# Square layers of a tiled attention and feed-forward kernel: a 16-bit low part, a power-of-two lift, and products of a kind in runs of 16

## Chip, cores and metric

The kernel runs on one core of a Trainium2 chip. The metric is the device time of one execution in microseconds; the kernel before was run three times: 905.81, 905.95 and 906.56 us, median 905.95.

## What is computed

Two blocks with residuals over x (32 sequences of 128 rows, 256 features): cross attention with 8 heads whose source is the normalised x and whose target is a context, then a feed-forward part whose weights hold only -1, 0 and 1 and a scale per output.

```python
x = x + xattn(ctx, layernorm(x), mask, mask, ...)          # all float32
def ffn(x):                                                # x: layernorm of the above, 256 features
    h = silu((x @ w1.T) * s1) * ((x @ w2.T) * s2)          # gates: 256 -> 1024
    h = gelu((h @ h1.T) * t1)                              # layer one:  1024 -> 1024
    h = gelu((h @ h2.T) * t2)                              # layer two:  1024 -> 1024
    return (h @ w3.T) * s3                                 # output: 1024 -> 256
x = x + ffn(layernorm(x))
```

## The kernel before

The sequences go through in 16 tiles of two, 256 rows each. Activations stand feature by row, so a product has a 128x128 block of a weight as the stationary operand and 128x256 of activations as the moving one; a layer of 1024 to 1024 is 8 output blocks of 8 steps. While tile f is in its feed-forward part, tile f+1 finishes its attention and f+2 starts it. The order of work is written out by hand for each engine (`tile`, `gates_part`, `middle_part`); tiles 1 to 12 are a hardware loop, tile 0 and tiles 13 to 15 stand apart. On TensorE a loop tile is: the four gate groups (`gate_up`), the projections of keys, queries and values of tile f+2 (L488, L506, L524), layer one, then attention, scores and output projection (L614, L542, L631), layer two, the output layer (`ffn_out`, L767). Engines meet by semaphores, whose targets `at` works out from the tile's number.

Since the weights are exact in few bits, float32 activations are kept by splitting them: VectorE casts a value to F32R (the high part, `hi`) and subtracts that from the value (the low part, `lo`). `split(f, q)` does this for a pair of 128x256 blocks, L1312 and L1314; q 0 to 3 is the gates' result, 4 to 7 layer one's, 8 to 11 layer two's. Each weight block is multiplied with both parts into one bank of PSUM. In the two square layers and the output layer both parts are F32R and alternate:

```python
for k in ks:
    part_product(mid_bank(f, q)[:, half, :], W, k, cols, hi, k == 0, False, general)
    ins = part_product(mid_bank(f, q)[:, half, :], W, k, cols, lo, False, k == KH - 1, general)
```

In the gates (L639, L640) the low part is F16 (`x2q`), multiplied with the upper 16 bits of each weight, two steps or four of a kind in a row; there the LayerNorm's result is 2**22 times too large, so that the low part keeps clear of F16's smallest values, and `gscols` takes it back. ScalarE does Silu (L891), Gelu (L898) and the exponentials (L926); GpSimd the power for LayerNorm and, at the start, casts of the weights. In tile 0 ScalarE also looks at every chunk of weights (L985) for bits below the 16th, and a flag chooses between the program above and one in float32 (`general`); with these inputs the first runs.

Of the kernel before, what the change touches and what calls it, by code (L numbers as in the profile page):

```python
# [19 lines left out]
LIFT = 2.0 ** 22  # L20
CH = 1024
# [11 lines left out]
    xt_done=1, k_done=2, q_done=1, v_done=1, xnT_ready=1, xnO_ready=1, kT_ready=2, qT_ready=2, vb_ready=1, v_ready=2,  # L33
# [8 lines left out]
def program(nc, x, ctxT, mask_row, mask_col, wsT, wvT, wtT, woT, first_rows, second_rows, x_mask_1, w1T, w2T, h1T, h2T,  # L42
            w3T, out):
    st = ExitStack()
    with st:
# [24 lines left out]
        neg_half = sb("neg_half", [P, NB])  # L70
# [27 lines left out]

        def turned(buf):

            return buf[:].rearrange("p c t -> p (c t)").rearrange("p (a c j i) -> p a c j i", a=ROWS, c=KD, j=NB)
# [5 lines left out]
        hAh, hAl = sb("hAh", [P, KH, T], F32R), sb("hAl", [P, KH, T], F32R)  # L107
# [6 lines left out]
        gscols = sb("gscols", [P, 2 * KH])  # L114

# [48 lines left out]
        def mid_bank(f, q):  # L164

            if q in (6, 10) and isinstance(f, int) and (f == TILES - 1 or f in (0, TILES - 2) and q == 6):
                return G[0][:].rearrange("p (h t) -> p h t", h=2)
            return F[q % 2][:]

# [64 lines left out]
        gscols_ready = sem("gscols_ready")  # L234
        gate_done = sem("gate_done")
# [81 lines left out]
        def _(sp):  # L317
# [54 lines left out]

            def store(f):
# [5 lines left out]
            def tile(f, a, m):  # L379
# [11 lines left out]
                if a is not None:  # L391
                    turn_x2(a)
                if m is not None:
                    turn_x(m)
# [62 lines left out]
        def _(pe):  # L457
# [248 lines left out]
            def middle_steps(f, q, half, ks, general):  # L706

                W, hi, lo = ((H1, H1_raw), hAh, hAl) if q < 8 else ((H2, H2_raw), hBh, hBl)
# [169 lines left out]
        def _(act):  # L878
            fn = nc.scalar.activation

            def silu(f, q):
# [105 lines left out]

            def tile(f, a, n):
# [54 lines left out]
            tile(0, 1, 2)  # L1043
            with act.Fori(1, TILES - 3) as i:
# [7 lines left out]
        def _(dve):  # L1052
# [232 lines left out]
            def gate_times_up(f, q):  # L1285
# [322 lines left out]
```

## Time and profile before

| | |
|---|---|
| median of three executions | 905.95 us |
| the profiled execution's own time | 906.56 us |
| its span, first to last instruction | 904.7 us |
| TensorE busy | 899.1 us, 99% |
| VectorE busy | 626.5 us, 69% |
| ScalarE busy | 390.6 us, 43% |
| GpSimd busy | 76.9 us, 8% |
| chain that ended last, by engine | PE 95%, DVE, DMA, POOL, ACT and issue 1% each |

The busy time of an engine counts its instructions, not its waits. The chain is followed back from the last instruction, at each step to what released it; its pieces on TensorE give the time that a run of products really takes, since single products overlap in the pipeline (one lasts some 280 ns and the next starts about 117 later).

### The profile page before, as it was taken

To read this page: it belongs to the slowest core of one execution; us is meant where nothing else is said; L and a number is where in the kernel's file an instruction comes from. 1 tells how busy PE (TensorE), PEld (TensorE's weight loads), DVE (VectorE), ACT (ScalarE), POOL (GpSimd) and SP (SyncE) were. 2 spreads that over 40 slices of the span, in tenths; PEclk is the share of its full clock that TensorE was granted. 3 is DMA by queue.
4 is the path that set the end of the run, shared out by engine and by line. 5 is a ranking of instruction groups with operands and counts; after the bars stand their busy time and mean duration, and the time that the engine had idled before them with its cause. 6 is when DMAs were issued, how large, how long until landed. Compare 5 with 4: busy or idle time off the path is not lost.

```text
span 904.7 us, 20863 instructions
## 1 busy us (share of the span) xinstructions
PE 899.1 (99%) x7600; PEld 853.8 (94%) x7600; DVE 626.5 (69%) x1256; ACT 390.6 (43%) x1101; POOL 76.9 (8%) x101
## 2 busy tenths in 40 slices
PE   9999999999999999999999999999999999999998
PEld 7799999999999999999999999999999999999998
DVE  5888858577585776858668586785857758586453
ACT  5973524425253252623535235253443525355231
POOL 3544000010000100001010000100001000000000
PEclk9999999999999999999999999999999999999999
DMA  9932232412214232142411424113241231303000
GB/s 347 385 116 57 75 81 62 122 56 85 74 46 122 65 100 60 36 122 70 119 37 35 122 70 122 39 55 98 70 122 47 75 87 54 94 24 106 24 13 14
DMA packets 82352, 79.27 MB, mean 88 GB/s; under 512 B 8592, under 2 KB 74896, under 8 KB 82320
## 3 DMA queue, kind: packets, MB, share of 16 engines
q1 hardware_dynamic: 81744, 78.31, 28.2%
q10 hardware_dynamic: 576, 0.52, 0.2%
q8 instruction: 21, 0.34, 0.2%
q14 instruction: 11, 0.09, 0.0%
HBM read 51.55 MB, written 27.26 MB: 87 GB/s over the span
## 4 chain that ended last, share of the span: by engine, by line
PE 95%; DVE 1%; DMA 1%; POOL 1%; ACT 1%; issue 1%; SPq 0%; DVEq 0%; POOLq 0%; ACTq 0%
PE F L646 50%; PE F L767 7%; PE G L631 6%; PE G L488 6%; PE G L524 5%; PE F L640 3%; PE G L640 3%; PE F L639 3%; PE G L639 3%; PE G L506 2%; PE S L542 2%; PE G L614 2%; PE G L646 1%; PE F L524 1%; DMA pr<-p_dram 0%
## 5 line engine op out<-in xcount | busy, mean ns | idle before, releaser
L898 ACT ACTIVATE g<-F,firsts 128x256 f32<-128x256 f32 x248 | 104.0, 472 | 320.6 <-PE F L646 317.7
L646 PE MATMUL F<-hBh,H 128*128 128x256 f32 x1008 | 239.5, 283 | 0.1
L646 PE MATMUL F<-hBl,H 128*128 128x256 f32 x1008 | 236.4, 279 | 0.0
L646 PE MATMUL F<-hAh,H 128*128 128x256 f32 x976 | 231.8, 282 | 0.0
L646 PE MATMUL F<-hAl,H 128*128 128x256 f32 x976 | 228.8, 279 | 0.0
L646 PEld LDWEIGHTS F<-hBl,H 128*128 128x128 f32 x1008 | 190.0, 188 | 0.4
L646 PEld LDWEIGHTS F<-hBh,H 128*128 128x128 f32 x1008 | 189.0, 187 | 0.7 <-ACT g L898 0.3
L646 PEld LDWEIGHTS F<-hAl,H 128*128 128x128 f32 x976 | 183.9, 188 | 0.4
L646 PEld LDWEIGHTS F<-hAh,H 128*128 128x128 f32 x976 | 183.0, 188 | 0.8 <-ACT sil L891 0.4
L1312 DVE CAST hBh<-g 128x512 fp32r<-128x512 f32 x64 | 28.1, 440 | 118.3 <-ACT g L898 118.3
L926 ACT ACTIVATE pr<-pr,nmx 128x128 f32<-128x128 f32 x240 | 92.7, 387 | 0.2
L1314 DVE TENSOR_TENSOR hAl<-g,hAh 128x512 fp32r<-128x512 f32 x128 | 88.6, 692 | 4.4
L1312 DVE CAST hAh<-g 128x512 fp32r<-128x512 f32 x128 | 54.9, 429 | 33.0 <-ACT g L898 31.8
L1479 POOL TENSOR_TENSOR rs<-ve,neg_half 128x2 f32<-128x2 f32 x15 | 10.4, 693 | 647.5 <-DVE ve L1246 647.5
L767 PE MATMUL F<-W,hAh 128*128 128x256 f32 x256 | 61.3, 281 | 0.0
L767 PE MATMUL F<-W,hAl 128*128 128x256 f32 x256 | 61.2, 280 | 0.0
L898 ACT ACT_TABLE_LOAD x17 | 21.8, 1283 | 76.6 <-PE F L646 76.6
L640 PE MATMUL F<-x2h,W 128*128 128x256 f32 x256 | 51.5, 302 | 0.5 <-DVE g L1293 0.5
L640 PE MATMUL G<-x2h,W 128*128 128x256 f32 x256 | 51.2, 301 | 0.0
L524 PE MATMUL G<-WV,cT 128*128 128x256 f32 x224 | 50.6, 379 | 0.0
L488 PE MATMUL G<-cT,WK 128*128 128x256 f32 x224 | 50.6, 379 | 0.0
L891 ACT ACTIVATE sil<-G,gscols 128x256 f32<-128x256 f32 x64 | 26.9, 471 | 53.4 <-PE G L640 53.4
(163 smaller groups left out, 1452.3 us busy)
## 6 DMA issues: line engine op xcount, KB each, us to landing
p_dram<-pb SPq DMA_DIRECT2D x30, 512.0 KB, 3.3
pr<-p_dram SPq DMA_DIRECT2D x120, 128.0 KB, 3.2
H_raw<-h SPq DMA_DIRECT2D x16, 512.0 KB, 14.5
cT<-ctx_t SPq DMA_DIRECT2D x14, 512.0 KB, 3.5
x_dram<-xt SPq DMA_DIRECT2D x28, 256.0 KB, 2.4
out<-y SPq DMA_DIRECT2D x32, 128.0 KB, 1.8
x_in<-x_t SPq DMA_DIRECT2D x15, 256.0 KB, 2.7
x2T<-x_dram SPq DMA_DIRECT2D x60, 64.0 KB, 1.9
```

The lines of the kernel that those rows point to most:

```text
L488: ins = mm(k_part(a, c), WK[:, k, c * P:(c + 1) * P], cT_of(a)[:, k, :], start=k == 0, stop=k == KC - 1)
L524: ins = mm(v_bank(a)[:, j * D:(j + 1) * D], cT_of(a)[:, k, j * P:(j + 1) * P], WV[:, k, :], start=k == 0, stop=k == KC - 1)
L631: ins = mm(G[1][:, j * D:(j + 1) * D], lhsT, WO[:, k, :], start=k == 0, stop=k == 2 * KD - 1)
L639: return mm(bank, high_halves(W[0])[:, k, cols], x2q[:, k, :], start=first, stop=last)
L640: return mm(bank, W[0][:, k, cols], x2h[:, k, :], start=first, stop=last)
L646: return mm(bank, W[0][:, k, cols], part[:, k, :], start=first, stop=last)
L767: ins = mm(F[j][:, 0, :], lhsT, W3[:, k, :], start=first, stop=last)
L891: fn(sil[:, p % 4, :], gate_bank[:, p % 2, :], ACT.Silu, scale=gscols[:, p:p + 1]).then_inc(sil_ready, 1)
L898: fn(g[:, q % 2, m, :], mid_bank(f, q)[:, m, :], ACT.Gelu, scale=scols[:, col:col + 1]).then_inc(gelu_ready, 1)
L926: ins = fn(pr[j][:, r, c, :], pr[j][:, r, c, :], ACT.Exp, bias=nmx[:, j, h:h + 1], scale=SCALE, accum_out=den[:, j, h:h + 1])
L1312: V.tensor_copy(hi[:, pair, :], g[:, q % 2, :, :]).then_inc(hi_ready, 1)
L1314: V.tensor_tensor(lo[:, pair, :], g[:, q % 2, :, :], hi[:, pair, :].bitcast(F32), ALU.subtract).then_inc(h_ready, 1)
```

## The change

In tiles 1 to 15 the low part of the two square layers is F16 (`hAq`, `hBq`) and is multiplied with the upper 16 bits of the weights. To keep it in range the layers' inputs are multiplied by powers of two: the gates' through the columns of scales that they are multiplied with anyway, layer one's by a multiplication of its own on VectorE ahead of each split (L1395), and Gelu's scales take both back (`lifted_cols`). The powers come from bounds that the kernel works out in tile 0: ScalarE squares and sums 12 chunks of weights, VectorE reduces these and the scales, the results go through memory to all partitions, and GpSimd and VectorE make the factors. Silu and Gelu write into `gA` and `gB`, which lie where `hAl` and `hBl` lie, instead of a ring of four and of two. The low and high steps of an output block are done in runs, and the order turns from block to block. Tile 0 and the output layer multiply as before.

```diff
+        hAh = sb("hAh", [P, KH, T], F32R)
+        hAl, gA = with_raw("hAl", KH, T)
         hBh, tile1_home = with_raw("hBh", KH, T)
-        hBl = sb("hBl", [P, KH, T], F32R)
-        g, sil = sb("g", [P, 2, 2, T]), sb("sil", [P, 4, T])
+        hBl, gB = with_raw("hBl", KH, T)
+        at_byte = -(-nc.sbuf_base // 32) * 32
+        hAq = sb("hAq", [P, KH, T], F16)
+        g = nc.alloc_sbuf_tensor_at("g", [P, 2, 2, T], F32, offset=at_byte)
+        hBq = sb("hBq", [P, KH, T], F16)
...
+        def g_pair(f, q):
+
+            if q >= 8 or is_first(f):
+                return g[:, q % 2]
+            return (gA, gB)[q // 4][:, 2 * (q % 4):2 * (q % 4) + 2, :]
...
+            def spread_sizes():
+
+                sp.wait_ge(sizes_ready, 3)
+                sp.dma_start(sizes_dram, sizes).then_inc(sizes_written, 16)
...
+                sp.dma_start(all_sizes, sizes_dram.rearrange("p n -> (p n)").unsqueeze(0).broadcast_to([P, 6 * P])).then_inc(sizes_loaded, 16)
...
-                for k in ks:
-                    if m == 0 and k % 2 == 0:
-                        pe.wait_ge(h_ready, at("h_ready", f, q - 4 + k // 2 + 1))
-                    cols = slice(m * P, (m + 1) * P)
-                    part_product(mid_bank(f, q)[:, half, :], W, k, cols, hi, k == 0, False, general)
-                    ins = part_product(mid_bank(f, q)[:, half, :], W, k, cols, lo, False, k == KH - 1, general)
...
+                else:
+                    lows = (half == 1, half == 0)
+                    for low in lows:
+                        for k in ks:
+                            first, last = low == lows[0] and k == 0, low == lows[1] and k == KH - 1
+                            if m == 0 and k % 2 == 0:
+                                done, name = (h_ready, "h_ready") if low else (hi_ready, "hi_ready")
+                                pe.wait_ge(done, at(name, f, q - 4 + k // 2 + 1))
+                            if low:
+                                ins = mm(bank, high_halves(W[0])[:, k, cols], low16[:, k, :], start=first, stop=last)
+                            else:
+                                ins = mm(bank, W[0][:, k, cols], hi[:, k, :], start=first, stop=last)
...
-                    if not isinstance(f, int):
-                        act.wait_ge(g_ready, at("g_ready", f, max(p - 3, 0)))
                     act.wait_ge(gate_done, at("gate_done", f, q + 1))
-                    if isinstance(f, int) and (f or p > 3):
-                        act.wait_ge(g_ready, at("g_ready", f, max(p - 3, 0)))
-                    fn(sil[:, p % 4, :], gate_bank[:, p % 2, :], ACT.Silu, scale=gscols[:, p:p + 1]).then_inc(sil_ready, 1)
+                    if is_first(f) and q > 1:
+                        act.wait_ge(h_ready, q - 1)
+                    fn(g_pair(f, q)[:, p % 2, :], gate_bank[:, p % 2, :], ACT.Silu, scale=gscols[:, p:p + 1]).then_inc(sil_ready, 1)
 
             def gelu(f, q):
-                act.wait_ge(h_ready, at("h_ready", f, q - 1))
+                if is_first(f) or q > 9:
+                    act.wait_ge(h_ready, at("h_ready", f, q - 1))
                 act.wait_ge(mid_done, at("mid_done", f, q - 3))
                 for m in (0, 1):
                     col = KH + 2 * q + m
-                    fn(g[:, q % 2, m, :], mid_bank(f, q)[:, m, :], ACT.Gelu,
-                       scale=scols[:, col:col + 1]).then_inc(gelu_ready, 1)
+                    scale = scols[:, col:col + 1] if is_first(f) else lifted_cols[:, col - KH:col - KH + 1]
+                    fn(g_pair(f, q)[:, m, :], mid_bank(f, q)[:, m, :], ACT.Gelu, scale=scale).then_inc(gelu_ready, 1)
...
+            def sum_squares(ns):
+
+                for n in ns:
+                    _, _, W = chunks[n]
+                    act.wait_ge(squares_ready, n)
+                    fn(y[:].rearrange("p j n -> p (j n)").bitcast(BF16)[:, 0:CH], W.rearrange("p k m -> p (k m)").bitcast(F32), ACT.Square,
+                       accum_out=squares[:, n:n + 1]).then_inc(squares_ready, 1)
...
+                    if first and q == 5:
+                        act.wait_ge(raw_loaded, 80)
+                    if first and q in (5, 6, 7):
+                        sum_squares(((0, 1), (2, 3), (4, 5))[q - 5])
...
+                    if first and q == 7:
+                        sum_squares(range(6, 10))
...
+                    if first and q == 8:
+                        sum_squares((10, 11))
...
+            act.wait_ge(lifted_cols_ready, 3)
...
-                dve.wait_ge(h_ready, at("h_ready", f, max(q - 1, 0)))
+                scales = gscols[:, KH:2 * KH] if is_first(f) else lifted_cols[:, 0:KH]
                 for p in (2 * q, 2 * q + 1):
+                    gate = g_pair(f, q)[:, p % 2, :]
                     dve.wait_ge(sil_ready, at("sil_ready", f, p + 1))
-                    V.scalar_tensor_tensor(g[:, q % 2, p % 2, :], up_bank[:, p % 2, :], gscols[:, KH + p:KH + p + 1],
-                                               sil[:, p % 4, :], ALU.mult, ALU.mult).then_inc(g_ready, 1)
+                    V.scalar_tensor_tensor(gate, up_bank[:, p % 2, :], scales[:, p:p + 1],
+                                               gate, ALU.mult, ALU.mult).then_inc(g_ready, 1)
...
+                if q < 8 and not is_first(f):
+                    lo = (hAq, hBq)[q // 4]
...
+                if 4 <= q < 8 and not is_first(f):
+                    V.tensor_scalar(whole_g, whole_g, lift[:, 1:2], None, ALU.mult).then_inc(in_lift, 1)
+                    dve.wait_ge(in_lift, at("in_lift", f - 1, q - 3))
+                V.tensor_copy(hi[:, pair, :], whole_g).then_inc(hi_ready, 1)
                 dve.wait_ge(hi_ready, at("hi_ready", f, q + 1))
-                V.tensor_tensor(lo[:, pair, :], g[:, q % 2, :, :], hi[:, pair, :].bitcast(F32),
+                V.tensor_tensor(lo[:, pair, :], whole_g, hi[:, pair, :].bitcast(F32),
...
+            def size_columns():
+
+                dve.wait_ge(squares_ready, BOUNDED)
+                gates = squares[:, 0:2 * KD].rearrange("p (w k) -> p w k", w=2)
+                V.tensor_reduce(sizes[:, 0:2], gates, AX.X, ALU.add).then_inc(sizes_ready, 1)
+                V.tensor_reduce(sizes[:, 2:3], squares[:, 2 * KD:], AX.X, ALU.add).then_inc(sizes_ready, 1)
...
+                V.tensor_reduce(sizes[:, 3:6], lifted_cols.rearrange("p (w k) -> p w k", w=3), AX.X, ALU.max).then_inc(sizes_ready, 1)
+
+            def lift_from_sizes():
+
+                dve.wait_ge(sizes_loaded, 16)
+                each = all_sizes.rearrange("p (s n) -> p n s", n=6)
+                V.tensor_reduce(whole[:, 0:3], each[:, 0:3], AX.X, ALU.add).then_inc(lift_steps, 1)
+                V.tensor_reduce(whole[:, 3:6], each[:, 3:6], AX.X, ALU.max).then_inc(lift_steps, 1)
...
+                V.tensor_tensor(whole[:, 0:3], whole[:, 0:3], whole[:, 3:6], ALU.mult).then_inc(whole_ready, 1)
+
+            def lift_columns():
+
+                dve.wait_ge(inverse_roots, 1)
+                V.scalar_tensor_tensor(lift[:, 0:1], whole[:, 3:4], ROOM / 16.0 ** 2, whole[:, 4:5], ALU.mult, ALU.mult).then_inc(lift_steps, 1)
...
+                V.tensor_scalar(lift.bitcast(I32), lift.bitcast(I32), 0x7F800000, None, ALU.bitwise_and).then_inc(lift_steps, 1)
...
+                V.tensor_scalar(lifted_cols[:, 0:KH], gscols[:, KH:2 * KH], lift[:, 0:1], None, ALU.mult).then_inc(lifted_cols_ready, 1)
...
+                V.tensor_scalar(lifted_cols[:, 2 * KH:3 * KH], scols[:, 3 * KH:4 * KH], unlift[:, 1:2], None, ALU.mult).then_inc(lifted_cols_ready, 1)
+                dve.wait_ge(lifted_cols_ready, 3)
...
                     mask_scores(n, 1)
+                if first:
+                    row_max(n, 1)
+                    size_columns()
                 split(f, 9)
...
                 split(f, 11)
-                if n is not None:
+                if first:
+                    lift_from_sizes()
+                elif n is not None:
                     row_max(n, 1)
                 scale_out(f, 0)
                 if a is None:
                     add_residual(f, 0)
                 scale_out(f, 1)
+                if first:
+                    lift_columns()
                 if a is not None:
...
+            pool.wait_ge(whole_ready, 1)
+            Gp.tensor_tensor(whole[:, 3:6], whole[:, 0:3], neg_half[:], ALU.pow).then_inc(inverse_roots, 1)
```

TensorE, entry into layer one of a loop tile, before (L646 is a product of either part; F0 is a PSUM bank, H1 the weights):

```order
L524 MATMUL G1<-WV,cT 128x256 x8
L688 REGISTER_ALU
L712 ISA
L646 MATMUL F0<-hAh,H1 128x256
L646 MATMUL F0<-hAl,H1 128x256
```

and now (L778 high, L776 low), from the last two steps of the first block's high run on:

```order
L778 MATMUL F0<-hAh,H1 128x256 x2
L776 MATMUL F0<-hAq,H1 128x256 x16
L778 MATMUL F0<-hAh,H1 128x256 x8
L778 MATMUL F1<-hAh,H1 128x256 x8
L776 MATMUL F1<-hAq,H1 128x256 x16
L778 MATMUL F1<-hAh,H1 128x256 x8
```

A pair of high and low, with a weight block loaded for each, has become 8 high, 16 low, 16 high and so on; the waits are on the high part first.

VectorE, the first split of layer one's result in a loop tile, before (L1312 the cast, L1314 the subtraction):

```order
L1197 STREAM_TRANSPOSE pb1<-pr1 128x8x4x32
L1305 REGISTER_ALU
L1306 ISA
L1312 CAST hBh<-g 128x512
L1313 REGISTER_ALU
L1314 TENSOR_TENSOR hBl<-g,hBh 128x512
```

and now (L1395 is the multiplication by the lift):

```order
L1276 STREAM_TRANSPOSE pb1<-pr1 128x8x4x32
L1387 REGISTER_ALU
L1388 ISA
L1395 TENSOR_SCALAR hBl_raw_58<-hBl_raw_58,small 128x512
L1396 ISA
L1397 CAST hBh<-hBl_raw_58 128x512
L1398 REGISTER_ALU
L1399 TENSOR_TENSOR hBq<-hBl_raw_58,hBh 128x512
```

One instruction and a wait on it stand ahead of the cast; the low part goes to `hBq`.

VectorE in tile 0, from split 8 to split 9, before (L1128 masks scores, L1063 begins tile 3's LayerNorm):

```order
L1314 TENSOR_TENSOR hAl<-g,hAh 128x512
L1128 TENSOR_TENSOR pr1<-S,mbias 128x1024
L1312 CAST hAh<-g 128x512
L1314 TENSOR_TENSOR hAl<-g,hAh 128x512
L1063 BN_STATS st1<-x_in 128x6 x2
```

and now (L1211 and L1215 are the maximum over scores, L1406 to L1410 `size_columns`):

```order
L1399 TENSOR_TENSOR hAl<-g_59,hAh 128x512
L1207 TENSOR_TENSOR pr1<-S,mbias 128x1024
L1211 TENSOR_REDUCE mx<-pr1 128x8
L1215 TENSOR_SCALAR nmx<-mx 128x8
L1406 TENSOR_REDUCE small<-small 128x2
L1407 TENSOR_REDUCE small<-small 128x1
L1408 TENSOR_TENSOR small<-firsts 128x24
L1410 TENSOR_REDUCE small<-small 128x3
L1397 CAST hAh<-g_59 128x512
L1399 TENSOR_TENSOR hAl<-g_59,hAh 128x512
```

The maximum over scores has moved here from behind split 11, where `lift_from_sizes` now stands, and four small instructions have come in between.

## Rows read from the trace of the kernel before

**Rows 1.** Page, totals: span, then busy us, share, instructions.

```profile
span 904.7 us, 20863 instructions
PE 899.1 (99%) x7600; PEld 853.8 (94%) x7600; DVE 626.5 (69%) x1256; ACT 390.6 (43%) x1101; POOL 76.9 (8%) x101
```

**Rows 2.** Chain that ended last, a loop tile: start us, us, what.

```profile
219.28 14.93 PE F L646 x128
...
239.97 14.94 PE F L646 x128
...
258.69 0.23 PE G L640 x2
258.92 0.45 PE G L639 x4
259.38 0.47 PE G L640 x4
...
266.10 3.45 PE G L488 x16
```

**Rows 3.** Line L639, the gates' low products: duration ns min/median/max.

```profile
L639 PEld LDWEIGHTS G<-x2q,W x256: 96/98/101, 34.1 to 864.8; 128*128 128x128 bf16 x128
L639 PE MATMUL G<-x2q,W x256: 272/273/284, 34.1 to 864.9; 128*128 128x256 f16 x128
```

**Rows 4.** Timeline of TensorE, two low products of a run: start, length.

```profile
96.34 0.38 PE L639 MATMUL G<-x2q,W 128*128 128x256 f16 x2
```

**Rows 5.** The chain in tile 14.

```profile
832.47 4.14 DMA pr<-p_dram
836.61 0.04 issue
836.66 0.65 PE G L614 x16
```

**Rows 6.** Timeline of VectorE, a loop tile; in brackets idle time before, releaser.

```profile
225.36 0.43 DVE L1312 CAST hBh<-g 128x512 fp32r<-128x512 f32 x1 [1.42 <-ACT g L898]
...
231.45 0.43 DVE L1312 CAST hBh<-g 128x512 fp32r<-128x512 f32 x1 [2.58 <-ACT g L898]
...
240.07 0.69 DVE L1237 TENSOR_TENSOR x<-G,xb 128x512 f32<-128x512 f32 x1 [0.99 <-PE G L631]
...
264.73 0.87 DVE L1293 SCALAR_TENSOR_TENSOR g<-G,gscols,sil 128x256 f32<-128x256 f32 x2
```

**Rows 7.** Groups of VectorE by line: busy us, mean ns, idle before.

```profile
L1078 DVE TENSOR_SCALAR xn<-x_in,mv,rs 128x256 f32<-128x256 f32 x30 | 11.0, 410 | 12.0 <-POOL rs L1467 12.0
L1246 DVE TENSOR_SCALAR ve<-mv 128x2 f32<-128x2 f32 x15 | 2.5, 170 | 1.6
L1160 DVE TENSOR_REDUCE mx<-pr 128x4 f32<-128x512 f32 x4 | 2.7, 686 | 0.1
L1263 DVE TENSOR_TENSOR x2l<-x2T,x2h 128x256 fp32r<-128x256 f32 x30 | 11.3, 420 | 0.0
L1263 DVE TENSOR_TENSOR x2q<-x2T,x2h 128x256 f16<-128x256 f32 x30 | 10.9, 404 | 0.1
```

**Rows 8.** Timeline of ScalarE, tile 0.

```profile
45.88 1.09 ACT L985 ACTIVATE look_out<-H_raw 128x1024 bf16<-128x1024 uint16 x1
...
77.45 0.84 ACT L898 ACTIVATE g<-F,firsts 128x256 f32<-128x256 f32 x2 [5.05 <-PE F L646]
```

**Rows 9.** Timeline of VectorE, tile 0 and the start of tile 1.

```profile
63.06 1.41 DVE L1314 TENSOR_TENSOR hBl<-g,hBh 128x512 fp32r<-128x512 f32 x1
...
81.02 1.22 DVE L1128 TENSOR_TENSOR pr<-S,mbias 128x1024 f32<-128x1024 f32 x1
...
89.98 0.69 DVE L1314 TENSOR_TENSOR hAl<-g,hAh 128x512 fp32r<-128x512 f32 x1
...
94.43 0.88 DVE L1293 SCALAR_TENSOR_TENSOR g<-G,gscols,sil 128x256 f32<-128x256 f32 x2 [0.51 <-PE G L640]
```

**Rows 10.** The chain in tile 0, its output layer.

```profile
88.55 3.78 PE F L767 x32
```

**Rows 11.** DMA issues: count, KB each, median us from issue to landing.

```profile
firsts<-mask_row SPq DMA_DIRECT2D x14, 128.0 KB, 3.2
```

More of the change, by code:

```diff
@@ L20 @@
 LIFT = 2.0 ** 22
+ROOM = 2.0 ** 26
+BOUNDED = 2 * KD + KH
 CH = 1024
@@ L69, in program @@
         ident = sb("ident", [P, P])
-        neg_half = sb("neg_half", [P, NB])
+        neg_half = sb("neg_half", [P, 3])
         act_set = sb("act_set", [P, 1])
@@ L97, in program @@
         x2_dram = nc.dram_tensor("x2_dram", (ROWS, P, KD * NB * DH), F32, kind="Internal").ap()
+        sizes_dram = nc.dram_tensor("sizes_dram", (P, 6), F32, kind="Internal").ap()
+        all_sizes = pb[0][:].rearrange("p s n -> p (s n)")[:, 0:6 * P]
         def turned(buf):
@@ L114, in program @@
         gscols = sb("gscols", [P, 2 * KH])
+        small = sb("small", [P, 3 * KH + BOUNDED + 16])
+        lifted_cols, squares = small[:, 0:3 * KH], small[:, 3 * KH:3 * KH + BOUNDED]
+        sizes, lift = small[:, 3 * KH + BOUNDED:3 * KH + BOUNDED + 6], small[:, 3 * KH + BOUNDED + 6:3 * KH + BOUNDED + 8]
+        unlift = small[:, 3 * KH + BOUNDED + 8:3 * KH + BOUNDED + 10]
+        whole = small[:, 3 * KH + BOUNDED + 10:3 * KH + BOUNDED + 16]
         cT_1 = tile1_home[:, 0:KC, :]
@@ L168, in mid_bank, with is_first @@
             return F[q % 2][:]
+        def is_first(f):
+            return isinstance(f, int) and f == 0
+        def g_pair(f, q):
+            if q >= 8 or is_first(f):
+                return g[:, q % 2]
+            return (gA, gB)[q // 4][:, 2 * (q % 4):2 * (q % 4) + 2, :]
         def sem(name):
@@ L234, in program @@
         gscols_ready = sem("gscols_ready")
+        squares_ready = sem("squares_ready")
+        sizes_ready = sem("sizes_ready")
+        scales_squared = sem("scales_squared")
+        sizes_written = sem("sizes_written")
+        sizes_loaded = sem("sizes_loaded")
+        whole_ready = sem("whole_ready")
+        inverse_roots = sem("inverse_roots")
+        lift_steps = sem("lift_steps")
+        lifted_cols_ready = sem("lifted_cols_ready")
+        in_lift = sem("in_lift")
         gate_done = sem("gate_done")
@@ L392, in tile @@
                     turn_x2(a)
+                if is_first(f):
+                    spread_sizes()
                 if m is not None:
@@ L706, in middle_steps @@
             def middle_steps(f, q, half, ks, general):
-                W, hi, lo = ((H1, H1_raw), hAh, hAl) if q < 8 else ((H2, H2_raw), hBh, hBl)
+                W, hi, lo, low16, whole_g = (((H1, H1_raw), hAh, hAl, hAq, gA) if q < 8 else ((H2, H2_raw), hBh, hBl, hBq, gB))
                 m = 2 * (q % 4) + half
-                for k in ks:
-                    if m == 0 and k % 2 == 0:
-                        pe.wait_ge(h_ready, at("h_ready", f, q - 4 + k // 2 + 1))
-                    cols = slice(m * P, (m + 1) * P)
-                    part_product(mid_bank(f, q)[:, half, :], W, k, cols, hi, k == 0, False, general)
-                    ins = part_product(mid_bank(f, q)[:, half, :], W, k, cols, lo, False, k == KH - 1, general)
+                cols = slice(m * P, (m + 1) * P)
+                bank = mid_bank(f, q)[:, half, :]
+                if is_first(f):
+                    for k in ks:
+                        if m == 0 and k % 2 == 0:
+                            pe.wait_ge(h_ready, at("h_ready", f, q - 4 + k // 2 + 1))
+                        part_product(bank, W, k, cols, hi, k == 0, False, general)
+                        ins = part_product(bank, W, k, cols, lo, False, k == KH - 1, general)
+                elif general:
+                    for k in ks:
+                        if m == 0 and k % 2 == 0:
+                            pe.wait_ge(h_ready, at("h_ready", f, q - 4 + k // 2 + 1))
+                        ins = mm(bank, W[1][:, k, cols], whole_g[:, k, :], start=k == 0, stop=k == KH - 1)
+                else:
+                    lows = (half == 1, half == 0)
+                    for low in lows:
+                        for k in ks:
+                            first, last = low == lows[0] and k == 0, low == lows[1] and k == KH - 1
+                            if m == 0 and k % 2 == 0:
+                                done, name = (h_ready, "h_ready") if low else (hi_ready, "hi_ready")
[4 more added lines that the diff above has]
+                                ins = mm(bank, W[0][:, k, cols], hi[:, k, :], start=first, stop=last)
                 if half and ks[-1] == KH - 1:
@@ L1306, in split @@
                     dve.wait_ge(mid_done, at("mid_done", f - 1, 8))
-                    if q == 4 and isinstance(f, int) and f == 0:
+                    if q == 4 and is_first(f):
                         dve.wait_ge(xb_ready, at("xb_ready", 1, 2))
```

23 lines of the change are left out of this document (18 added, 5 removed).

## The prediction

> **What bounds the kernel.** I read the page's totals first, then the chain that ended last in order of time, then single instructions of TensorE, and last the idle times of VectorE and ScalarE around the places the change touches. The totals: TensorE is busy 899.1 of 904.7 us, VectorE 626.5, ScalarE 390.6 [rows 1]. The chain of a loop tile is TensorE without a break: layer one is one piece of 128 products in 14.93 us, 116.6 ns a product, layer two the same [rows 2]. So a saving on TensorE counts in full until another engine is late, and a delay elsewhere counts only beyond its spare time.
>
> **The saving.** In layers one and two of tiles 1 to 15 half of the products, 64 of 128 in each layer, become what the gates' low products (L639) already are: 16-bit weights against an F16 part, 256 columns. Their price is in the trace. Four high and four low ones alternate there, and the 64 products of a tile's gates take from 258.69 to 266.10, so 7.41 us or 115.8 ns each [rows 2]. That is only 0.8 ns under the all-F32R layer, so the mean over the gates says that almost nothing is gained. Inside a run it is different: two following low products span 0.38 us (rounded) and one lasts 273 ns, so they start some 109 ns apart [rows 3, 4]. Eight products of the gates take 0.926 us; four at 109.2 and four at 116.6 would be 0.903. The rest, 23 ns, is what one pair of switches (high to low and back) costs. The new order makes runs of 16, so four pairs of switches in a layer:
> 64 x 116.6 + 64 x 109.2 + 4 x 23 = 14.54 us against 14.93, a gain of 0.385 us a layer. From below, with the gates' mean, it would be 128 x 0.8 = 0.1 us; from above, without switches, 0.47. I take 0.385, since the spacing inside a run is a direct reading.
>
> Thirty layers change. The first layer of tile 14 gains nothing: behind it TensorE already waits for a transfer of probabilities that ends at 836.61 [rows 5], and that transfer hangs on exponentials that don't move. Tile 15 takes three banks together in its layers and so has some 12 low runs instead of 4; 8 more pairs leave it 0.2 us a layer. Sum: 27 x 0.385 + 2 x 0.2 = 10.8 us.
>
> The Trainium skill has another figure for this ("TensorE: Matmul & The Clock Gate", section on the back-to-back issue gap): in a sustained stream of weight loads and products it gives about 81 ns for 128 columns and 131 for 512, by a straight line some 98 ns for 256, an estimate. The 109 ns read here disagree for runs of four; for runs of 16 no row here speaks. By it the time would be that of the second rival below.
>
> **What VectorE pays in each tile.** Four multiplications by the lift, 128x512 in place, one before each split of layer one's result. A CAST of that shape takes 0.43 us [rows 6], a multiplication with scalars read per partition 0.41 for half the columns [rows 7]: so between 0.43 and 0.82; I take 0.7, nearer to the second, its own kind. The first of them finds 1.42 us of idle time before the CAST [rows 6], the next two likewise wait for a Gelu. The last one delays what is queued behind it on VectorE, the masking of scores and their maximum, by 0.7, and these end in 0.99 us of waiting for the output projection (L1237) [rows 6]. So the LayerNorm behind it starts as before, with 0.3 to spare (at 0.82 still 0.2). Layer two begins only after attention, scores and output projection, so that its parts come in time; high first asks for pair 3 after 6 products instead of 12, 0.7 us sooner, but masking and maximum, 1.2 us each [rows 9], lie between the last split and the 0.99 us, so that split ends some 3.6 us before layer two starts and with the lift still 2.9. Cost: nothing. Without that cover the last lift of a tile would count, 0.7 x 15 = 10.5 us.
>
> The low parts are written as F16 instead of F32R: 404 against 420 ns in the same subtraction of the x2 parts [rows 7], nothing. Silu into the layer's own buffer takes waits off ScalarE and VectorE that nobody waited on.
>
> **What tile 0 pays once.** ScalarE squares 12 chunks of 1024; the look at a chunk, the same shape with the same kind of sum, is 1.09 us plus its read-out [rows 8], so about 1.3, since each now waits for the one before. They stand in groups of 2, 2, 2, 4, 2 behind Gelus; the largest, 5.2 us, goes into 5.05 us of idle [rows 8]. Nothing, or 0.2 for a Gelu that TensorE needs much later. The order shows no further table load.
> VectorE pays more. It runs without a gap from 81.02 to the first gate product of tile 1 at 94.43, before which it idles 0.51 us [rows 9]. Into this stretch go 15 instructions: 13 tiny ones and two reductions of 3x128. A tiny one is 170 ns and some 50 between two that depend, say 0.22 [rows 7]; a reduction of 512 elements is 686 ns [rows 7], so one of 384 about 0.55. 13 x 0.22 + 2 x 0.55 = 4.0 us. The maximum over scores that moves ahead of split 9 (1024 elements, so about 1.2 us, and a tiny one) adds nothing to this total but brings 1.4 us of it forward. Felt first: the low part of split 11 ends at 90.67 [rows 9], now near 92.9; the output layer starts at 88.55 and asks for it after 24 of its 32 products of 118 ns [rows 10], at 91.4, so TensorE waits 1.5 us there. The rest is felt in tile 1: its gates go on into the key projection only when the third pair of gate products is made; in a loop tile this is ready at 265.60 and asked for at 266.10 [rows 2, 6], 0.5 spare. Total: 4.0 - 0.5 - 0.5 = 3.0 us on the path, 1.5 of it in tile 0. The sizes travel through memory meanwhile: a broadcast of 128 KB lands in 3.2 us [rows 11], so two transfers from 84.4 on are back by about 91.5, before 92.9; the queued transfer of tile 3's x behind them waits for VectorE longer than for them. The power on GpSimd (0.7) lies beside the two output scalings. Bounds: 0, if VectorE's idle and the two waits overlap better than I think, and 5, if the strided reductions run at half speed.
>
> **Sum.** Against the profiled execution (906.56 us, span 904.7): 906.56 - 10.8 + 3.0 = 898.8. This execution is 0.6 above the median of the runs shown, so I say 898.2.
>
> **Rivals.**
> First, nothing of tile 0 reaches the path: 895.2. For it speaks only that most edges of this kernel are covered; against it, the gapless VectorE of [rows 9].
> Second, in a long run the low products are paced by their weight load, 98 ns [rows 3], not by 109: 64 x 11 = 0.7 us more in each of 29 layers, 20.5 in all, 877.7. Against it, the third and fourth product of a run are already 109 apart, and the load is already shorter than that.
> Third, the change doesn't give what it says: the loss in the gates belongs to mixing and not to switches, each product gains 0.8 ns only, 29 x 0.1 = 3 us, eaten by tile 0: 905.9, no change. For it, the 115.8; against it, the starts inside a run.
> Fourth, the slower side: the row of gate products and splits on VectorE in front of the key projection. It has 0.5 us to spare, and the change rewrites every instruction in it (gate product in place, low part in another type). Should the two low parts in it slow down as one did beside GpSimd's casts, 1.41 instead of 0.69 [rows 9], TensorE would wait 1.44 - 0.5 = 0.94 us in each of 13 tiles, 12.2 in all: 910.4. It makes the kernel slower from 1.1 us of growth on, (10.8 - 3.0) / 13 + 0.5. Against it, the F16 row of 404 ns, and GpSimd is idle in that stretch of a loop tile.
>
> **Chances.** Forecast 0.70, with its own range 896 to 901; first rival 0.09, second 0.05, third 0.09, fourth 0.05, and 0.02 for some other loss. A difference under 0.2%, 1.8 us, can't be told from none. Faster by more: the forecast, the first two: 0.84 or a little more; within 0.2%: the third, 0.09, slower 0.07. The range 894.5 to 902.5 holds the forecast with both ends of tile 0's cost and the first rival; the other three lie outside.
>
> **What would show it.** In the changed profile layer one of a loop tile should be a piece of about 14.54 us, and the tile 54.7 instead of 55.45. Starts in a low run should be 109 ns apart; 116 would mean the third rival, 98 the second. The four lifts should last about 0.7 us and the wait for L1237's successor shrink from 0.99 to about 0.3, not to zero. TensorE should wait some 1.5 us in tile 0's output layer and another 1.5 between the gates and the key projection of tile 1, and in no later tile; waits there in every tile would be the fourth rival. The forecast is wrong if the switches cost more in long runs, or if VectorE's row gets longer than its spare time.

## The result, and the profile after

| | before | after |
|---|---|---|
| median of four executions | 906.22 us | 900.83 us (900.41 to 900.83) |
| ratio | | 0.994, 95% interval 0.9922 to 0.9957 |
| the profiled execution's span | 904.7 us | 899.1 us |

The kernel is 5.4 us faster, at 900.8; 898.2 was forecast. The changed kernel's page, span and busy times, against [rows 1]:

```profile
span 899.1 us, 20745 instructions
PE 889.7 (99%) x7600; PEld 816.9 (91%) x7600; DVE 658.7 (73%) x1331; ACT 404.9 (45%) x1125; POOL 78.0 (9%) x102
```

TensorE runs as many products as before and is busy 9.4 us less, VectorE is busy 32 us more. The chain that ended last, in a loop tile of the changed kernel (start, length, instructions), against [rows 2]:

```profile
222.82 0.93 PE F L778 x8
223.75 1.76 PE F L776 x16
225.51 1.87 PE F L778 x16
...
236.42 0.94 PE F L778 x8
237.36 1.01 PE G L658 x32
...
257.68 3.79 PE F L830 x32
...
268.89 3.45 PE G L532 x16
```

L778 are the high products, L776 the low ones. A layer goes from 222.82 to 237.36, 14.54 us. Sixteen high ones take 1.87 us, 116.9 ns each, sixteen low ones 1.76. TensorE's timeline has one such low run as a single row, to set beside [rows 4]:

```profile
223.59 1.92 PE L776 MATMUL F<-hAq,H 128*128 128x256 f16 x16
```

One product lasts 273 ns, so the 15 steps between starts are (1.92 - 0.273) / 15 = 109.8 ns. The pace of some 109 read from runs of four holds in runs of sixteen, and a whole loop tile, from one key projection to the next, takes 54.70 us instead of 55.45. VectorE in the same tile, against [rows 6]:

```profile
227.47 0.49 DVE L1395 TENSOR_SCALAR hBl_raw<-hBl_raw,small 128x512 f32<-128x512 f32 x1
227.99 0.43 DVE L1397 CAST hBh<-hBl_raw 128x512 fp32r<-128x512 f32 x1
...
238.27 0.49 DVE L1395 TENSOR_SCALAR hBl_raw<-hBl_raw,small 128x512 f32<-128x512 f32 x1 [1.96 <-ACT hBl_raw L961]
...
243.22 0.69 DVE L1316 TENSOR_TENSOR x<-G,xb 128x512 f32<-128x512 f32 x1 [0.68 <-PE G L675]
```

The lift (L1395) takes 0.49 us, and the wait ahead of L1316 (L1237 before) shrinks from 0.99 to 0.68 and is still there. So the loop does what was forecast; the difference lies in tile 0. TensorE's waits of the changed kernel (engine, line, what it waited for: us in total, times, longest):

```profile
PE G L684 <- ACT hAl_raw L952: 1.5, 1, 1.5
...
PE F L690 <- issue: 0.9, 1, 0.9
PE F L830 <- DVE hAl L1399: 0.8, 1, 0.8
PE F L684 <- DVE g L1373: 0.6, 1, 0.6
...
PE G L532 <- DVE hAl_raw L1373: 0.5, 1, 0.5
```

Each stands there once. The 0.6 at L684 lies in tile 0's own gates, and the kernel before has it too (0.55 us, L640). The others are new: layer one of tile 0 (L690), its output layer (L830), the third gate group of tile 1 (L684, 1.5) and its key projection (L532). The first of these was not forecast at all, and between tile 1's gates and key projection stand 2.0 us instead of 1.5. ScalarE in and behind tile 0 shows where they come from:

```profile
44.14 0.84 ACT L952 ACTIVATE g<-F,gscols 128x256 f32<-128x256 f32 x2 [1.46 <-DVE hAl L1399]
...
62.84 1.07 ACT L1055 ACTIVATE y<-W 128x1024 bf16<-128x1024 f32 x1
...
97.85 1.28 ACT L952 ACT_TABLE_LOAD   x1 [6.92 <-DVE small L1436]
99.15 0.84 ACT L952 ACTIVATE hAl_raw<-G,gscols 128x256 f32<-128x256 f32 x2
```

First, tile 0's Silu now waits 1.46 us for a split (`act.wait_ge(h_ready, q - 1)`): it writes into the ring of two that the gate products use, where before it had a ring of four. The looks at the weights queue behind it. Second, the table load of Silu stands behind the new wait for `lifted_cols`, and its 1.28 us begin when VectorE is through. The Silu at 99.15 is that of tile 1's first pair; the third gate group writes the bank that it reads, and so waits for it. VectorE there, against [rows 9]:

```profile
51.72 0.17 DVE L1454 TENSOR_REDUCE low_most<-low_bits 128x1 f32<-128x22 f32 x1 [1.16 <-ACT look_out L1047]
52.32 0.14 DVE L1458 TENSOR_SCALAR flag<-most 1x1 int32<-1x1 f32 x1 [0.42 <-POOL most L1617]
...
92.89 0.69 DVE L1399 TENSOR_TENSOR hAl<-g,hAh 128x512 fp32r<-128x512 f32 x1
93.50 0.86 DVE L1416 TENSOR_REDUCE small<-pb 128x3 f32<-128x384 f32 x1
94.28 0.86 DVE L1417 TENSOR_REDUCE small<-pb 128x3 f32<-128x384 f32 x1
...
97.44 0.22 DVE L1436 TENSOR_SCALAR small<-firsts,small 128x8 f32<-128x8 f32 x1
...
99.66 0.88 DVE L1373 SCALAR_TENSOR_TENSOR hAl_raw<-G,small,hAl_raw 128x256 f32<-128x256 f32 x2 [0.73 <-ACT hAl_raw L952]
```

The flag, by which TensorE chooses its program ahead of layer one, comes at 52.32 because the last look comes late; in the kernel before it came 1.2 us sooner:

```profile
51.12 0.14 DVE L1336 TENSOR_SCALAR flag<-most 1x1 int32<-1x1 f32 x1 [0.42 <-POOL most L1488]
```

Behind the last split come two reductions of 0.86 us each and a string of tiny instructions; then VectorE waits 0.73 us for the Silu that stood behind the table load.

### The profile page after: what moved, and what is told of

It is laid out like the page before. It is cut to its first block, busy times and chain, and to the rows that moved or that the text cites. A ratio compares the mean times of both kernels' runs of the same rounds, so it can differ in the third digit from the quotient of the medians.

```text
span 899.1 us, 20745 instructions
## 1 busy us (share of the span) xinstructions
PE 889.7 (99%) x7600; PEld 816.9 (91%) x7600; DVE 658.7 (73%) x1331; ACT 404.9 (45%) x1125; POOL 78.0 (9%) x102
## 4 chain that ended last, share of the span: by engine, by line
PE 89%; DVE 5%; issue 2%; DMA 2%; POOL 1%; ACT 1%; SPq 0%; DVEq 0%; POOLq 0%; ACTq 0%
PE F L778 24%; PE F L776 22%; PE F L830 6%; PE G L675 6%; PE G L532 5%; PE G L568 5%; PE G L684 3%; PE F L684 3%; PE G L683 3%; PE F L683 3%; PE G L550 2%; PE S L586 2%; PE G L658 2%; DMA pr<-p_dram 1%; DMA p_dram<-pb 1%
## 5 line engine op out<-in xcount | busy, mean ns | idle before, releaser
L961 ACT ACTIVATE g<-F,small 128x256 f32<-128x256 f32 x118 | 49.7, 472 | 198.7 <-PE F L778 198.7
L778 PE MATMUL F<-hBh,H 128*128 128x256 f32 x944 | 131.5, 288 | 0.0
L778 PE MATMUL F<-hAh,H 128*128 128x256 f32 x928 | 130.7, 288 | 0.0
L961 ACT ACTIVATE hBl_raw<-F,small 128x256 f32<-128x256 f32 x116 | 48.8, 472 | 171.1 <-PE F L778 171.1
L778 PEld LDWEIGHTS F<-hBh,H 128*128 128x128 f32 x944 | 117.0, 188 | 1.7 <-ACT hBl_raw L961 0.3
L778 PEld LDWEIGHTS F<-hAh,H 128*128 128x128 f32 x928 | 115.4, 188 | 1.9 <-ACT hAl_raw L952 0.4
L776 PE MATMUL F<-hBq,H 128*128 128x256 f16 x944 | 114.4, 273 | 0.0
L776 PE MATMUL F<-hAq,H 128*128 128x256 f16 x928 | 113.5, 273 | 0.0
L776 PEld LDWEIGHTS F<-hBq,H 128*128 128x128 bf16 x944 | 87.3, 98 | 11.9
L776 PEld LDWEIGHTS F<-hAq,H 128*128 128x128 bf16 x928 | 85.4, 98 | 11.7
L1395 DVE TENSOR_SCALAR hBl_raw<-hBl_raw,small 128x512 f32<-128x512 f32 x60 | 29.2, 487 | 86.9 <-ACT hBl_raw L961 86.9
L830 PE MATMUL F<-W,hAh 128*128 128x256 f32 x256 | 61.6, 281 | 0.8 <-DVE hAl L1399 0.8
L830 PE MATMUL F<-W,hAl 128*128 128x256 f32 x256 | 61.4, 281 | 0.0
L684 PE MATMUL G<-x2h,W 128*128 128x256 f32 x256 | 51.3, 302 | 1.5 <-ACT hAl_raw L952 1.5
L684 PE MATMUL F<-x2h,W 128*128 128x256 f32 x256 | 51.5, 302 | 0.6 <-DVE g L1373 0.6
L532 PE MATMUL G<-cT,WK 128*128 128x256 f32 x224 | 50.7, 379 | 0.5 <-DVE hAl_raw L1373 0.5
L830 PEld LDWEIGHTS F<-W,hAh 128*128 128x128 f32 x256 | 48.3, 189 | 1.0 <-DVE hAl L1399 1.0
```

The lines of the kernel that those rows point to most:

```text
L532: ins = mm(k_part(a, c), WK[:, k, c * P:(c + 1) * P], cT_of(a)[:, k, :], start=k == 0, stop=k == KC - 1)
L684: return mm(bank, W[0][:, k, cols], x2h[:, k, :], start=first, stop=last)
L776: ins = mm(bank, high_halves(W[0])[:, k, cols], low16[:, k, :], start=first, stop=last)
L778: ins = mm(bank, W[0][:, k, cols], hi[:, k, :], start=first, stop=last)
L830: ins = mm(F[j][:, 0, :], lhsT, W3[:, k, :], start=first, stop=last)
L961: fn(g_pair(f, q)[:, m, :], mid_bank(f, q)[:, m, :], ACT.Gelu, scale=scale).then_inc(gelu_ready, 1)
```

## Experiments

Theory: tile 0's cost has three separate causes (Silu's wait, the table load behind a wait, the bounds on VectorE), and in the loop the gain is the type of the low part, less a price per switch. To see a stage and not only a total, the start of each product is compared with the start of the product of the same number before (7600 in each record; only inside a block of the square layers does their order differ). The differences in us:

| place, by the clock of before | after | e1 | e2 | e3 | e10 | e11 | e7 |
|---|---|---|---|---|---|---|---|
| tile 0, gates, 34 | -0.06 | -0.47 | 0.08 | 0.11 | -0.15 | -0.07 | -0.34 |
| tile 0, layer one, 54 | 1.05 | -0.49 | 1.34 | 0.10 | -0.14 | -0.05 | -0.35 |
| tile 0, layer two, 80 | 1.44 | -0.66 | 1.24 | -0.01 | -0.37 | -0.21 | -0.26 |
| tile 1, first gates, 94 | 2.50 | 0.43 | 2.33 | 1.07 | -0.13 | -0.21 | -0.26 |
| tile 1, last gates, 98 | 4.27 | 2.16 | 2.85 | 1.62 | 1.11 | 1.00 | -0.26 |
| tile 1, key projection, 102 | 5.06 | 2.95 | 4.02 | 2.79 | 2.28 | 2.18 | -0.26 |
| from layer two, 80, to key projection, 102 | 3.62 | 3.61 | 2.78 | 2.80 | 2.65 | 2.39 | 0.00 |
| last layer, 901 | -5.64 | -8.12 | -6.92 | -7.86 | -8.76 | -8.84 | -11.29 |

The first row scatters by 0.6 us with the loads at the start, and is no effect of an edit. The stretch from 54 to 80 scatters as well: the kernel after, e4, e5 and e6, which do the same there, differ from before by -0.04 to 0.39 us in it, so nothing in it is put down to an edit. The last row but one leaves it out; there kernels that do the same agree within 0.04 us (3.60 to 3.64 in the kernel after, e1, e4, e5 and e6). Each column is one profiled execution. The ratios below have intervals of about ±0.0014, or 1.3 us; of steps smaller than that this table speaks, not the ratio.

**e1_silu.** Silu of tile 0 gets a place of its own; the gate product writes into the ring and waits there itself.

```diff
-                    if is_first(f) and q > 1:
-                        act.wait_ge(h_ready, q - 1)
-                    fn(g_pair(f, q)[:, p % 2, :], gate_bank[:, p % 2, :], ACT.Silu, scale=gscols[:, p:p + 1]).then_inc(sil_ready, 1)
+                    fn(gA[:, p, :], gate_bank[:, p % 2, :], ACT.Silu, scale=gscols[:, p:p + 1]).then_inc(sil_ready, 1)
```

> Against the changed kernel's 900.8 us, of which 5.1 us are tile 0's extra cost. Theory (three causes add): Silu of tile 0 waits for the split of the pair before, because it writes into the ring of two that the gate products use; with a place of its own layer one of tile 0 starts 1.1 to 1.2 us sooner (52.2 instead of 53.4 on the profile's clock), and the kernel takes 899.7. Rival (one cause): all of the 5.1 us come from the row of bounds on VectorE at the end of tile 0, which only pushes what is late already; the earlier start is eaten there and the time stays 900.8.

898.65 us, ratio 0.9922 (0.9908 to 0.9936). Layer one of tile 0 starts with no delay against its own gates (first two rows of the table); the chain that ended last has it without a wait:

```profile
49.94 2.16 PE G L568 x10
52.09 3.97 PE F L690 x34
```

This cause is real, 1.1 us at the start of layer one, and it is not eaten later: from layer two on e1 loses as much as the kernel after (3.61 and 3.62). The key projection is 1.7 us better, both counted from the gates of tile 0; the other 0.56 appears from 54 to 80, where the kernel after and e2, both starting layer one late, differ by 0.5 among themselves, so that part can't be given to the edit. Nor can the 0.4 us that e1 gains more behind tile 1. These two are most of what its time fell (2.2 us) beyond the theory's 1.1.

**e2_wait.** ScalarE's wait moves to the first instruction that needs it.

```diff
             def gelu(f, q):
+                if q == 4 and not is_first(f):
+                    act.wait_ge(lifted_cols_ready, 3)
...
             tile(0, 1, 2)
-            act.wait_ge(lifted_cols_ready, 3)
```

> ScalarE's wait for the lifted columns moves from ahead of tile 1 to the first Gelu of layer one, which is the first to read them; Silu's table load (1.28 us, at 97.85 in the changed kernel) can then run while VectorE still works on the bounds. Theory: the third gate product of tile 1 starts when VectorE is through, 98.9 instead of 99.66, so 0.7 us less, 900.1. Rival: the load counts in full, 1.3 to 1.7 less, 899.3. Second rival (bounds on VectorE alone decide): nothing, 900.8.

899.83 us, ratio 0.9935 (0.9921 to 0.9949). From tile 0's gates to the key projection it loses 3.94 us instead of 5.12, 1.2 less; but part of that lies in the stretch that scatters. From layer two on, where the edit acts, it is 2.78 instead of 3.62: 0.84 less, near the theory's 0.7. (The gate product at 99.66 is tile 1's first, not its third.) **e3_both**, both edits:

> Both edits. If the causes add: 900.8 - 1.1 - 0.7 = 898.9. If the row on VectorE takes back what the earlier start gives: 900.1.

898.37 us, ratio 0.9917 (0.9903 to 0.9931). Its table load, on ScalarE's timeline, now runs as soon as the last Gelu is done, and the first pair of Silu waits only for its gates; VectorE goes into the gate products without a gap:

```profile
89.50 1.28 ACT L950 ACT_TABLE_LOAD   x1
94.36 0.84 ACT L950 ACTIVATE hAl_raw<-G,gscols 128x256 f32<-128x256 f32 x2 [3.58 <-PE G L684]
```

```profile
97.05 0.43 DVE L1136 COPY res<-x 128x512 f32<-128x512 f32 x1
97.39 0.87 DVE L1373 SCALAR_TENSOR_TENSOR hAl_raw<-G,small,hAl_raw 128x256 f32<-128x256 f32 x2
```

From layer two of tile 0 to the key projection e3 loses 2.80 us. Against e1 (3.61) the table load is worth 0.81, against 0.84 without e1's edit: the two causes add. What is left should be the bounds.

**e7_const.** Both edits, and no bounds at all.

> Both edits, and the bounds are left out: no squares, no reductions, no trip through memory, no power; the lift is the constant 1, and its columns are written in idle time of VectorE before tile 0's last split of layer one. The work in the loop is unchanged. Theory: tile 0's whole extra cost goes (5.1 us) and the steady gain of 10.7 stays: 895.6 to 896. Rival: part of the 5.1 us is not in these three places (another wait, or the ring's new place): 897.5 or more.

895.32 us, ratio 0.9882 (0.9866 to 0.9898). From the gates of tile 0 to the key projection it loses 0.08 us, and from layer two on 0.00: nothing of tile 0's cost lies outside the three causes. The bounds, with their squares on ScalarE, their trip and the power on GpSimd, are worth 2.8 us from layer two on. From there to the last layer it gains 11.03 us, the kernel after 10.70; the kernels with the same loop lie between 10.65 (e3) and 11.07 (e1), so the 0.3 lies within their scatter.

**e4_alternate.** High and low products in turn, nothing else changed.

```diff
-                    for low in lows:
-                        for k in ks:
+                    for k in ks:
+                        for low in (False, True):
```

> Only the order inside an output block of layers one and two (tiles 1 to 14) is changed: high, low, high, low instead of a run of eight of each; the products, their types and all else stay. A pair of switches then comes with every pair of products, 64 a layer instead of 4. Theory (a switch between kinds costs, 23 ns a pair): a layer takes 64 x (116.6 + 109.2 + 23) = 15.93 us instead of 14.54, worse than before's 14.93; over 28 layers and some 29 with tile 15 that is 39 us, so about 940. Rival (the two kinds have a price of their own and their mixing costs a fixed 0.8 ns short of the old pace, as the mean over the gates reads): 14.82 a layer, 909. Second rival (16-bit products save 7.4 ns each whatever the order): 14.45 a layer, 900 or less.

934.56 us, ratio 1.0314 (1.0298 to 1.033): slower than before. TensorE's timeline, two high products with a low one between, and layer two's first product with the one that follows the layer:

```profile
248.30 0.47 PE L777 MATMUL F<-hBh,H 128*128 128x256 f32 x1
...
248.65 0.36 PE L777 MATMUL F<-hBh,H 128*128 128x256 f32 x1
248.86 0.28 PE L775 MATMUL F<-hBq,H 128*128 128x256 f16 x1
248.90 0.36 PE L777 MATMUL F<-hBh,H 128*128 128x256 f32 x1
...
264.12 0.37 PE L829 MATMUL F<-W,hAh 128*128 128x256 f32 x1
```

A pair takes 0.25 us, and the layer 264.12 - 248.30 = 15.82 us. In the kernel after the same layer, between the same two places, is 14.74 (242.78 to 257.52 on its timeline):

```profile
242.78 0.82 PE L778 MATMUL F<-hBh,H 128*128 128x256 f32 x4
...
257.52 0.28 PE L830 MATMUL F<-W,hAh 128*128 128x256 f32 x1
```

Layer one grows by 1.17, layer two by 1.07: 1.12 on the mean for 60 more pairs of switches, 18.7 ns a pair. The mechanism is the forecast's, its price is 18.7 and not 23; both rivals (909, 900) fall. The order alone decides between gaining 5 us and losing 28.

**e5_runs_f32r.** Runs as after, but the low part is F32R and the weights whole.

```diff
-     ins = mm(bank, high_halves(W[0])[:, k, cols], low16[:, k, :], start=first, stop=last)
+     ins = mm(bank, W[0][:, k, cols], lo[:, k, :], start=first, stop=last)
```

> The runs stay, but the low part of the square layers is F32R again and multiplied with the whole weights; lift and bounds stay. Theory (the type of the low part gives the gain, runs alone give nothing, because products of one type need no switch): 14.93 us a layer, 900.8 + 29 x 0.385 = 912. Rival (runs of a kind give the gain in any type, since the same part stays the moving operand): about 901.

911.49 us, ratio 1.0062 (1.0047 to 1.0078). The chain that ended last has low (L776) and high (L778) runs of one length:

```profile
224.99 1.87 PE F L776 x16
226.85 1.87 PE F L778 x16
```

Runs alone give nothing: from first product to first product behind a layer it is 15.21 and 15.13 us, as before. What is left against before, 5.3 us, is tile 0's cost (4.97 by the starts, gates to key projection) with no gain to pay it. The edit changes the type of both operands of a low product; which of the two gives the gain was not tested.

**e6_no_lift.**

> The multiplication by the lift ahead of each split of layer one's result is left out, 60 instructions of 0.487 us on VectorE; the rest stays. Theory (all of it lies in spare time): within 0.2% of 900.8. Rival (the last lift of a tile delays the LayerNorm and what follows): 15 x 0.3 to 0.5 = 4.5 to 7 us less, 894 to 896.

900.34 us, ratio 0.9942 (0.9926 to 0.9957), the same as after. On VectorE the wait returns to the 0.99 of [rows 6], and nothing comes of it:

```profile
242.90 0.69 DVE L1316 TENSOR_TENSOR x<-G,xb 128x512 f32<-128x512 f32 x1 [0.99 <-PE G L675]
```

**e9_trim.** Meant as a better version: from e3, sizes taken in idle time, the second maximum behind the last split again, reductions over whole stretches.

```diff
-                sp.dma_start(sizes_dram, sizes).then_inc(sizes_written, 16)
+                sp.dma_start(sizes_dram.rearrange("n p -> p n"), sizes, allow_slow_non_contiguous=True).then_inc(sizes_written, 16)
...
-                each = all_sizes.rearrange("p (s n) -> p n s", n=6)
+                each = all_sizes.rearrange("p (n s) -> p n s", n=6)
```

> Against the version with both edits (Silu's own place, the wait at the first Gelu), 898.4 us, whose remaining cost of tile 0 is some 2.7 us. The sizes of the columns are taken in VectorE's 0.8 us of waiting ahead of the LayerNorm's scaling of tile 2's x (0.44 us off the row), and go to memory feature by feature, so that the two reductions of 3x128 read whole stretches instead of every sixth element (0.86 us each now; the rows of a reduction over whole stretches give about 0.55, so 0.6 off). The second maximum over scores goes back behind the last split. Theory (VectorE's row from the last split to tile 1's gate products is without a gap, so each us off it is a us of the time): 898.4 - 1.1 = 897.3. Rival (a reduction takes 2.2 ns an element however it reads): 898.0. Second rival (writing the sizes element by element is slow enough for VectorE to wait for the trip): 899 or more.

905.3 us, ratio 0.9992 (0.9983 to 1.0001): the second rival, far beyond its 899. The DMA issues between 84 and 97 us (KB each, us to landing), e9 first, the kernel after second, and e9's VectorE:

```profile
sizes_dram<-small SPq DMA_DIRECT2D x1, 3.0 KB, 9.2
```

```profile
sizes_dram<-small SPq DMA_DIRECT2D x1, 3.0 KB, 2.4
```

```profile
100.45 0.55 DVE L1416 TENSOR_REDUCE small<-pb 128x3 f32<-128x384 f32 x1 [7.97 <-DMA pb<-sizes_dram]
100.92 0.54 DVE L1417 TENSOR_REDUCE small<-pb 128x3 f32<-128x384 f32 x1
```

The 3 KB, written 4 bytes at a time, land after 9.2 us instead of 2.4, and the broadcast behind them after 5.2 us instead of 3.1, so VectorE waits 8 us. The Trainium skill has the rule ("DMA: Bandwidth & Descriptors", rules for kernel authors): a last dimension with gaps in it becomes one descriptor per element and is better rearranged. The trace agrees: between 84 and 97 us e9 has 848 packets under 512 bytes, the kernel after 304. The small packets themselves are through by 87.6, though; what fills the time until they count as landed, at 95.2, is not shown. The reductions themselves came down to 0.55 us, so stride made up the rest of the 0.86. TensorE waits too, and its granted clock falls (its waits, then the clock and two low runs of tile 1's gates):

```profile
PE F L684 <- DVE y L1444: 7.5, 1, 7.5
```

```profile
99.20:105.90 6.70, 3.72 (x17) 3.19 (x18) 4.94 (x18) 0.84 (x2) 0.85 (x1) 0.50 0.41 125
```

```profile
102.75 1.08 PE L683 MATMUL F<-x2q,W 128*128 128x256 f16 x4
...
106.10 0.61 PE L683 MATMUL G<-x2q,W 128*128 128x256 f16 x4
```

Idle from 94.65 to 102.18, TensorE is granted 0.50 of its clock, 1.2 instead of 2.4 GHz, from 99.1 to 105.9, and four low products take 1.08 us instead of 0.61. A gate group there takes 3.60 us, in e10 1.92. Here this is covered: the key projection still waits 0.3 us for VectorE, whose row the trip has made late.

**e10_idle, e11_sums.** e9 with the trip as it was; then also the sums over partitions on ScalarE (`fn(each[:, n], each[:, n], ACT.Copy, accum_out=whole[:, n:n + 1])` ahead of its loop).

> The trimmed version again with its trip through memory as it was (partition by partition, 2.4 us to land instead of the 9.2 us that VectorE waited for last time). Against the version with both edits, 898.4 us, only the place on VectorE differs: the sizes of the columns (0.44 us) are taken in its wait ahead of the scaling of tile 2's x, and the second maximum goes back behind the last split. Theory (VectorE's row up to tile 1's key projection has no gap, each us off it is a us of the time): 898.4 - 0.4 = 898.0, and TensorE's wait in tile 0's output layer (0.8) goes, to come back at the key projection. Rival (the wait in the output layer is lost by itself, and moving the maximum behind it wins it back): 897.5 or less. Second rival (the trip is late again): 899 or more.

> As the run beside it, and the sums over all partitions are taken by ScalarE (three in-place copies with a sum, in its 3.6 us of idle time ahead of tile 1's first Silu), so that one strided reduction of 0.86 us leaves VectorE. Theory (unit slope): 0.8 to 0.9 less than the run beside it, 897.1. Rival (Silu's table load now stands behind the sums and comes too late for the first Silu): as the run beside it or slower, 898 to 899.

897.9 us, ratio 0.9908 (0.9893 to 0.9923), and 897.59 us, ratio 0.9906 (0.9891 to 0.9921): the fastest that compute everything, though not told apart from e3 or from each other by their ratios. From layer two of tile 0 to the key projection e10 loses 2.65 us, 0.15 less than e3; of the 0.44 taken off, 0.32 came back as a wait of VectorE for a Gelu. The wait in the output layer went (tile 1's first gates at -0.13 instead of 1.07) and came back at the gates and the key projection, as the theory said. e11 gains 0.26 more instead of 0.8. Its VectorE and ScalarE:

```profile
88.18 0.76 DVE L1345 TENSOR_TENSOR x2q<-x2T,x2h 128x256 f16<-128x256 f32 x2 [0.51 <-ACT x2h L1039]
...
93.10 0.17 DVE L1423 TENSOR_TENSOR small<-small 128x3 f32<-128x3 f32 x1 [0.32 <-ACT pb L1125]
```

```profile
93.08 1.28 ACT L950 ACT_TABLE_LOAD   x1
94.38 0.84 ACT L950 ACTIVATE hAl_raw<-G,gscols 128x256 f32<-128x256 f32 x2
```

Of the 0.86 us that left VectorE, 0.32 came back as a wait for the sums. The wait of 0.51 for a part of x2 lies ahead of the sums and is not theirs: ScalarE got to that part late, after 1.87 us of waiting for a transfer. The later table load was feared and is harmless: VectorE comes to that Silu's result only at 96.78. So "each us off the row is a us of the time" holds only until VectorE meets what it now waits for.

## Why the prediction was right, and where its size was off

**The saving was right.** From tile 1's key projection to the last layer the kernel gains 5.06 + 5.64 = 10.70 us; "10.8 us" was forecast. The layer is 14.54, as worked out, and the tile 54.7. The starts 109.8 ns apart rule out the second rival (98 ns), and e4 and e5 rule out the third: the gain is the type's, the loss is the switches'. The price of a pair, "23 ns", measured 18.7 and hardly mattered at four pairs a layer.

**The lifts were right in effect, too dear in size.** Forecast 0.7 us, measured 0.49, close to the CAST's 0.43 that was the lower bound. The nearest row of "its own kind" (410 ns for half the columns, [rows 7]) has two scalars per partition and was the worse guide. The Trainium skill ("VectorE: DVE Perf Modes", the perf-mode tier table) puts multiplication by a scalar and copy of float32 in SBUF into one class, and the trace agrees for one scalar with 487 ns on the mean beside 431; the row with two does not fit the class. e6 shows that they cost nothing.

**VectorE's bounds were right in sum, in part by luck.** Forecast 4.0 us of instructions; on the trace they are 0.44 for the sizes (85.05 to 85.49), 1.8 from the first reduction to the next output scaling, and 1.4 from 96.30 to 97.70 with 0.27 of waiting ahead, 3.9. The two parts were off in opposite ways: a reduction took 0.86 and not 0.55, because its elements lie six apart; a tiny instruction took less than 0.22. On the path "3.0 us" were forecast, and e3 less e7 gives 2.8 from layer two on.

**The term that was mis-sized is the total for tile 0**, "3.0 us on the path", which measured 5.1: 1.1 for Silu's wait, 0.8 for the table load, 2.8 for the bounds, and 0.4 in the stretch that scatters. Two sentences hid the first two. "Silu into the layer's own buffer takes waits off ScalarE and VectorE that nobody waited on" is true of tiles 1 to 15; in tile 0 Silu goes into the ring and gets a new wait, and 1.1 us of that reaches TensorE through the looks, the flag and the branch (e1). "The order shows no further table load" is true, but the one that was there moved behind a wait, and that is 0.8 us (e2, and e3 against e1). By the starts, the two savings add. In tile 0's output layer 0.8 us of waiting came instead of 1.5. The fourth rival did not come: TensorE waits for gate products in tile 1 alone.

Not settled: what makes the stretch from 54 to 80 scatter by 0.4 us, and the gain behind tile 1 by as much.

## What to carry to other kernels

When two kinds of products share TensorE, read the spacing inside a run and the mean over a mixed stretch; their difference is the price of switching, and it says whether an order will pay before anything is built. When a wait is added, list what stands behind it in that engine's queue, a table load and a flag included, and do so for the first tile on its own, since it often takes another branch. Put a wait at the first instruction that needs its result.

## What the runs showed that was not expected

- Alternating F32R and 16-bit products cost 18.7 ns per pair of switches, which makes the mixture slower (15.82 us a layer) than F32R alone (15.13, between the same places).
- A reduction of 3x128 float32 takes 0.86 us with its elements 24 bytes apart and 0.55 over whole stretches.
- 3 KB written to memory in 4-byte pieces land after 9.2 us, in pieces of 24 bytes after 2.4 us, though the packets were through by 87.6, within 1.6 us of the issue at 86.0.
- TensorE, idle for 7.5 us in e9, was granted 0.50 of its clock from 99.1 to 105.9, and a gate group took 3.60 us instead of 1.92.
- An in-place multiplication of 128x512 float32 by one scalar per partition takes 0.49 us; with two scalars 128x256 takes 0.41 [rows 7].
